# Experts' second products channel-major with the bias in the eviction, and a tail that multiplies by gates spread over the partitions

## What is computed

```python
t = _to_tokens(x)                       # (16, 1024, 128)
t = t + _L0_ffn_ref(_ln_t(t), ...)
...
h = (x_flat @ W_gat).reshape(M, HEADS, NUM_EXPERTS)
...                                     # softmax over each token's edges, sum of the sources' rows
scores = _layernorm(agg, ln_gamma, ln_beta).reshape(M, HEADS, NUM_EXPERTS).mean(1)
topk_s, topk_i = jax.lax.top_k(scores, TOP_K)      # 2 of 4
w = jax.nn.softmax(topk_s, axis=-1)
for ei in range(NUM_EXPERTS):
    g = jnp.where(topk_i == ei, w, 0.0).sum(-1)
    hh = jax.nn.gelu(x @ W1[ei] + b1[ei], approximate=False)
    out = out + g[..., None] * (hh @ W2[ei] + b2[ei])
```

## Time and profile before

| | us |
|---|---|
| timed runs, median of 3 | 4056.19 (4053.61 to 4056.93) |
| profiled execution, first to last instruction | 4750.1 |
| block 1, in the profiled execution | 0 to 2370 |
| block 2, the experts' part and the last rounds | 2370 to 4593 |
| block 3, the gates | 4593 to 4642 |
| block 3, the tail | 4642 to 4750 |

### The profile page before, as it was taken

How to read it: one execution, slowest core, us unless ns; L and a number is a source line. 1 busy time by engine, 2 the same in 40 slices (tenths; PEclk the granted TensorE clock), 3 DMA queues, 4 the chain that set the end, 5 groups by cost and what they waited for, 6 DMA issues and landing times. The chain is left out here.

```text
span 4750.1 us, 30403 instructions
## 1 busy us (share of the span) xinstructions
PE 2949.0 (62%) x8964; PEld 1485.1 (31%) x8964; DVE 3244.3 (68%) x5382; ACT 1526.0 (32%) x2234; POOL 1184.2 (25%) x1252
## 2 busy tenths in 40 slices
PE   6987889999989998866603444334433443345207
PEld 3433333444434443334401222222222222122107
DVE  7899688888887988776445555555544555557587
ACT  2331254444544544455301222212211112112107
POOL 0000000000000000111175445444445555554400
PEclk9989989999999999977756666666566666667559
DMA  4113224544545463856511111111101111011127
GB/s 168 62 58 122 79 72 128 176 147 143 183 123 183 157 209 125 267 185 214 143 17 23 31 31 31 31 31 31 31 22 31 25 31 32 23 14 13 32 109 275
DMA packets 336048, 452.11 MB, mean 95 GB/s; under 512 B 80429, under 2 KB 251832, under 8 KB 326922
## 3 DMA queue, kind: packets, MB, share of 16 engines
q1 hardware_dynamic: 289722, 390.77, 25.2%
q0 software_dynamic: 46160, 59.39, 5.5%
HBM read 340.18 MB, written 109.85 MB: 95 GB/s over the span
## 5 line engine op out<-in xcount | busy, mean ns | idle before, releaser
L1554 POOL DMA_INDIRECT got<-scratch_tab,src_at x1120 | 1065.1, 951 | 341.3 <-issue 341.3
L1508 PE MATMUL hid_ps<-tokens,w 128*128 128x512 f32 x512 | 336.6, 793 | 1068.5 <-ACT hid L1832 580.1
L699 PE MATMUL in_ps<-tokens,w_in 128*128 128x512 f32 x2048 | 939.8, 611 | 24.5 <-ACT zst L906 19.8
L699 PEld LDWEIGHTS in_ps<-tokens,w_in 128*128 128x128 f32 x2048 | 394.8, 197 | 507.6 <-issue 507.6
L1508 PEld LDWEIGHTS hid_ps<-tokens,w 128*128 128x128 f32 x512 | 114.2, 247 | 1192.8 <-ACT hid L1832 604.7
L716 PE MATMUL out_ps<-w_out,act 128*128 128x512 f32 x1024 | 475.7, 608 | 3.9 <-DMA w_out<-in_m_WoutT 3.9
L626 POOL MEMSET tokens<- 1x128 int32 x1 | 0.2, 195 | 1905.6 <-DVE tokens L1098 1905.6
L1097 DVE TENSOR_TENSOR tokens<-tokens 128x1024 f32<-128x1024 f32 x380 | 465.2, 1224 | 11.2 <-ACT tokens L864 10.2
L1524 PE MATMUL y_ps<-w,hid 128*128 128x128 f32 x2048 | 331.0, 314 | 225.5 <-issue 222.0
L1098 DVE TENSOR_TENSOR tokens<-tokens 128x1024 f32<-128x1024 f32 x380 | 464.9, 1224 | 0.0
L1824 ACT ACTIVATE ys<-y_ps 128x512 f32<-128x512 f32 x128 | 76.5, 597 | 1156.5 <-remote 819.5
(11 more groups left out here) (325 smaller groups left out, 4291.7 us busy)
## 6 DMA issues: line engine op xcount, KB each, us to landing
w_out<-in_m_WoutT SPq DMA_DIRECT2D x256, 512.0 KB, 4.5
w_in<-in_m_WinT SPq DMA_DIRECT2D x128, 512.0 KB, 3.9
scratch_y<-ys SPq DMA_DIRECT2D x25, 1024.0 KB
got<-scratch_tab,src_at POOLq DMA_INDIRECT x1120
tokens<-scratch_xt SPq DMA_DIRECT2D x8, 2048.0 KB, 10.0
scratch_sz<-zst SPq DMA_DIRECT2D x64, 256.0 KB, 4.6
gz<-scratch_sz SPq DMA_DIRECT2D x64, 256.0 KB, 4.7
ys<-scratch_y SPq DMA_DIRECT2D x9, 1024.0 KB, 11.6
```

What stands on the lines that cost most here:

```text
L699: last = t_.matmul(in_ps[:, z, :], w_in[:, n % WIN, k, :], xT[:, s % 2, k, :], start=(k == 0), stop=(k == KC - 1))
L1508: last = t.matmul(hid_ps[:, f], w1[:, e, f * P:(f + 1) * P], tokens[:, g * QW:(g + 1) * QW], start=True, stop=True)
L1554: g.indirect_dma_start(got[:, y, t, :], None, tab_d[:, :], bass.IndirectOffsetOnAxis(ap=src_at[:, y, t:t + 1], axis=0))\
```

## The change

In block 2 the second product is turned round. `w2` becomes the stationary operand and the 512 tokens of `hid` the moving one: two matmuls of 512 columns per unit, with channels on the partitions. The bias matmul goes, and `b2`, now one number to a partition, is added by ScalarE's eviction. Nothing else in block 2 changes.

In block 3 the experts' outputs are channel-major already, and the gates must be the same on all partitions and different along the tokens. VectorE splits `by_expert` into three bf16 parts that add up to it (`parts`), SP moves them in twelve DMAs of 32 partitions, so that the gates of 32 chunks lie on 96 partitions (`by_chunk`), and TensorE makes them into `g_ps` per chunk: one bf16 matmul whose stationary operand is a column of `pick`, repeated 128 times, which picks one chunk's three parts, adds them and writes the result to all partitions. VectorE multiplies a whole quarter of four experts in place by `g_ps` (one operation of 128x2048), GpSimd adds the halves in place (experts 0, 1 to 2, 3: 128x1024), VectorE adds the two quarters left into `ost`, then `x2g`. ScalarE has no part in the tail any more. `g_ps` has two places, so TensorE runs two quarters ahead, and VectorE's multiplication too.

```diff
@@ block 2
-            b2 = sb("b2", [1, EXP, P], F32, st)
+            b2 = sb("b2", [P, EXP], F32, st)
...
-                sp.dma_start(b2[:], a["b2"].rearrange("(o e) d -> o e d", o=1)).then_inc(s_mw, 16)
+                with nc.allow_non_contiguous_dma(reason="small parameters, one to a partition"):
+                    sp.dma_start(b2[:], a["b2"].rearrange("e d -> d e")).then_inc(s_mw, 16)
...
-                    t.matmul(y_ps[:, n % 2], ident[0:1, 0:1].to_broadcast([1, P]),
-                             b2[:, e, :].unsqueeze(1).to_broadcast([1, QW // P, P]), start=True, stop=False)
                     t.wait_ge(s_gelu, n + 1)
-                    for c in range(QW // P):
-                        for f in range(FH):
-                            last = t.matmul(y_ps[:, n % 2, c * P:(c + 1) * P], hid[:, n % 2, f, c * P:(c + 1) * P],
-                                            w2[:, e, f, :], start=False,
-                                            stop=(c == QW // P - 1 and f == FH - 1))
+                    for f in range(FH):
+                        last = t.matmul(y_ps[:, n % 2], w2[:, e, f, :], hid[:, n % 2, f], start=f == 0,
+                                        stop=f == FH - 1)
...
-                        s.activation(ys[:, g % SLOTS, e], y_ps[:, n % 2], ACT.Copy).then_inc(s_yc, 1)
+                        s.activation(ys[:, g % SLOTS, e], y_ps[:, n % 2], ACT.Identity,
+                                     bias=b2[:, e:e + 1]).then_inc(s_yc, 1)
@@ block 3, SyncE
-                            sp.wait_ge(s_mix, CH * (q - R + 1))
+                            sp.wait_ge(s_read, q - R + 1)
...
+                sp.wait_ge(s_part, 1)
+                for k in range(P // GROUP):
+                    for x in range(3):
+                        sp.dma_start(by_chunk[x * GROUP:(x + 1) * GROUP, k], parts[k * GROUP:(k + 1) * GROUP, x])\
+                            .then_inc(s_chunk, 16)
@@ block 3, TensorE
...
+                t.wait_ge(s_chunk, 16 * 3 * (P // GROUP))
                 for q in range(NQ_ALL):
                     if q >= 2:
-                        t.wait_ge(s_fin, q - 1)
...
+                        t.wait_ge(s_scaled, q - 1)
                     for c in range(CH):
...
+                        k, i = divmod(CH * order[q] + c, GROUP)
+                        last = t.matmul(g_ps[:, q % 2, c, :], pick[:, i:i + 1].to_broadcast([3 * GROUP, P]),
+                                        by_chunk[:, k, :], start=True, stop=True)
+                    last.then_inc(s_g, 1)
@@ block 3, GpSimd (new)
+                for q in range(NQ_ALL):
+                    y = rings[q % R].rearrange("p (x n) -> p x n", x=2)
+                    g.wait_ge(s_scaled, q + 1)
+                    g.tensor_tensor(y[:, 0], y[:, 0], y[:, 1], ALU.add).then_inc(s_halved, 1)
@@ block 3, VectorE, after the gates
...
+                ck(v.tensor_copy(parts[:, 0], gate))
+                ck(v.tensor_tensor(rest, gate, parts[:, 0], ALU.subtract))
+                ck(v.tensor_copy(parts[:, 1], rest))
+                v.tensor_tensor(parts[:, 2], rest, parts[:, 1], ALU.subtract).then_inc(s_part, 1)
+
+                def scaled(q):
                     if q < NQ_ALL:
...
+                        y = rings[q % R].rearrange("p (e c n) -> p c e n", e=EXP, n=P)
+                        on_chip(v, q)
+                        v.wait_ge(s_g, q + 1)
+                        v.tensor_tensor(y, y, g_ps[:, q % 2].rearrange("p c (e n) -> p c e n", n=P),
+                                        ALU.mult).then_inc(s_scaled, 1)
+
+                scaled(0)
+                scaled(1)
+                for q in range(NQ_ALL):
+                    y = rings[q % R].rearrange("p (e n) -> p e n", e=EXP)
+                    v.wait_ge(s_halved, q + 1)
+                    if q >= 4:
+                        v.wait_ge(s_out[q % 4], 16 * (q // 4))
+                    v.tensor_tensor(ost[:, q % 4, :], y[:, 0], y[:, 1], ALU.add).then_inc(s_read, 1)
+                    scaled(q + 2)
+                    v.wait_ge(s_read, q + 1)
+                    v.wait_ge(s_xg[q % RES], 16 * (q // RES + 1))
+                    v.tensor_tensor(ost[:, q % 4, :], ost[:, q % 4, :], x2g[:, q % RES, :], ALU.add).then_inc(s_fin, 1)
```

More of the change, by code:

```diff
@@ L137 @@
 CH = QW // P
+GROUP = 32
 def image_end(n):
@@ L1924, in program @@
             wide = [P, BINS, H16]
+            agg_n = agg_f.rearrange("p n x -> p (n x)")
+            parts = agg_n[:, 0:3 * QW // 2].bitcast(BF16).rearrange("p (x n) -> p x n", x=3)
+            by_chunk = agg_n[0:3 * GROUP, 3 * QW // 2:7 * QW // 2].bitcast(BF16).rearrange("p (k n) -> p k n", n=QW)
+            rest = e_score[:].rearrange("p n e -> p (n e)")
             found_f = found.rearrange("p n x -> p (n x)")
@@ L1993, in _ @@
                 s.activation(e_score[:], e_score[:], ACT.Exp).then_inc(s_na, 1)
-                s.wait_ge(s_gt, 1)
-                s.activation(g_tok[:], g_ps[:], ACT.Copy).then_inc(s_gt, 1)
-                s.wait_ge(s_gt, 2)
-                for q in range(NQ_ALL):
-                    y = rings[q % R].rearrange("p (e n) -> p e n", e=EXP)
-                    if q >= SLOTS:
-                        s.wait_ge(s_ring[q % R], 16 * (q // R + (1 if q % R >= SLOTS else 0)))
-                    for c in range(CH):
-                        n = CH * q + c
-                        j = CH * order[q] + c
-                        if n >= 8:
-                            s.wait_ge(s_mix, n - 7)
-                        s.activation(first2[:, n % 8], y[:, 0, c * P:(c + 1) * P], ACT.Copy, scale=g_tok[:, 0, j:j + 1])\
-                            .then_inc(s_first2, 1)
-                        s.activation(third[:, n % 8], y[:, 2, c * P:(c + 1) * P], ACT.Copy, scale=g_tok[:, 2, j:j + 1])\
-                            .then_inc(s_da, 1)
             @block.vector
@@ L2023, in _ @@
                     v.memset(rank[:, :, i:i + 1], float(EXP - 1 - i))
+                for x in range(3):
+                    at = slice(x * GROUP, (x + 1) * GROUP)
+                    ck(v.tensor_copy(pick[at, :], ident[at, at]))
                 v.wait_ge(s_nw, 48)
@@ L2070, in _ @@
                 ck(v.reciprocal(vec[1][:], vec[0][:]))
-                v.tensor_tensor(by_expert[:].rearrange("p e n -> p n e"), gates[:], spread(vec[1][:], EXP),
-                                ALU.mult).then_inc(s_nv, 1)
-                v.wait_ge(s_gt, 2)
-                def fourths(q):
-                    if q < NQ_ALL:
-                        y = rings[q % R].rearrange("p (e c d) -> p e c d", e=EXP, d=P)
-                        if q >= SLOTS:
-                            v.wait_ge(s_ring[q % R], 16 * (q // R + (1 if q % R >= SLOTS else 0)))
-                        if q >= 2:
-                            v.wait_ge(s_mix, CH * (q - 1))
-                        j = CH * order[q]
-                        v.tensor_tensor(fourth[:, q % 2].rearrange("p (c d) -> p c d", d=P), y[:, 3],
-                                        g_tok[:, 3, j:j + CH].unsqueeze(2).to_broadcast([P, CH, P]),
-                                        ALU.mult).then_inc(s_four, 1)
@@ new lines, in _ @@
+                ck(v.tensor_tensor(by_expert[:].rearrange("p e n -> p n e"), gates[:], spread(vec[1][:], EXP), ALU.mult))
+                gate = by_expert[:].rearrange("p e n -> p (e n)")
+                ck(v.tensor_copy(parts[:, 0], gate))
[3 more added lines that the diff above has]
+                def scaled(q):
+                    if q < NQ_ALL:
+                        y = rings[q % R].rearrange("p (e c n) -> p c e n", e=EXP, n=P)
[3 more added lines that the diff above has]
+                                        ALU.mult).then_inc(s_scaled, 1)
```

57 lines of the change are left out of this document (13 added, 44 removed).

## The result

The changed kernel takes **4138.57 us** (median; 4135.04 to 4142.39), the kernel before on the same chip 4054.9 (4051.0 to 4056.93). The ratio is 1.0209, 95% interval 1.0196 to 1.0222: 83.7 us slower. The forecast was 91 us slower, 4147 with a range of 4080 to 4165.

What follows compares the result with a forecast made beforehand. Timed loop turns were taken as bound by GpSimd's gathers (82.6 us), so the experts gain 0. A tail start 10 us later and a pace of 5.85 us a quarter add 91 to 4056: 4147 us, range 4080 to 4165.

Steps and rivals of the forecast that it cites:

- 664 of 694 us: Loop and last rounds: gather-bound timed turns of 82.6 us would explain 664 of the 694 us between profiled span and median.
- The experts' part: Loop: 166 us less TensorE work hides under the gathers, and at most 10 us more ScalarE eviction is hidden: 0.
- Rival (b): Loop: experts partly hold timed turns, so the change gains there; 4021 us if a turn were 90; chance 0.10.
- The start: Tail: splitting gates, twelve DMAs and landing put the first multiplication 10 us after the present first product.
- S(0): Tail: S is VectorE's multiplication by the gates; S(0), the first quarter's, was forecast at 4654 us.
- Rival (c): Start of tail: the twelve small DMAs come late once, 10 us on top, 4157 us; chance 0.68 shared with the forecast.
- The pace: Tail: VectorE waiting for GpSimd's addition makes a quarter take 5.85 us, against 2.68 before.
- P: Tail: GpSimd's addition of 128x1024 halves, forecast at 2.35 us a quarter and to go first.
- F: Tail: VectorE's sum with x2g, 0.69 us alone, forecast to wait for GpSimd's addition and last near 3.0.
- A: Tail: VectorE's sum of two halves, 128x512, forecast at 0.69 us, queued behind the sum with x2g.
- the earlier trace: First part: VectorE's addition began 0.23 us before GpSimd's of 2.35, yet lasted 3.14 instead of 0.685.
- Rival (a): Tail: VectorE passes GpSimd twice in a row; pace 3.45, or 3.96 in 17 refilled quarters; +30, 4086 us; chance 0.18.

Runs made afterwards that it cites:

- the kernel before once more: The kernel before, unchanged, profiled a second time: 4050.2 us (one run).
- P after F(q-2): Changed kernel, but GpSimd's addition of halves also waits for VectorE's sum with x2g of two quarters earlier: 4074.9 us, ratio 1.0067.
- P after A: Changed kernel, but GpSimd's addition of halves also waits for VectorE's sum of two halves of the quarter before: 4085.1 us, ratio 1.0070.

## Why the prediction was right, and where it wasn't

**The loop.** The conclusion from 664 of 694 us was right: timed turns are bound by the gathers (82.3 us after, 82.05 in the kernel before once more, 82.6 forecast), and the slow issue belonged to one execution. The experts' part was costed at 0 and measured 1.0002. Each part of the cover was there too: the eviction with a bias takes 0.69 instead of 0.60 and is hidden. Rival (b), that the experts hold a timed turn, is excluded from both sides: 191 us less work for TensorE (166 in the prediction) and 171 us more of it change nothing that can be told from noise. That the profiled turn would shrink "towards 100" was too careful: the slow issue simply didn't come again, and the profiled span of after is the timed one.

**The start.** Forecast 12.1 us from the gates to S(0), measured 13.2. The split took 2.4 instead of 2.8. The twelve issues took 7.55 where I chose 4.6: I had the row for it, 0.6 an issue, and discounted it for the smaller transfers, but these small ones cost 0.63 each. The landing took 1.9 instead of 3.24, 1.3 of it behind the last issue. That the errors nearly cancel is luck. Rival (c) didn't come.

**The pace.** This is the step that was wrong, in its detail and not in its kind. I let P win before F, with F stretched to 3.0 and A free; 5.85 us a quarter. In the trace F passes with 0.68, P waits for it, and A is stretched to 2.83; 5.55. From the quarter shown: S to F 2.19, F 0.68, from F's end to P's 2.20, A's end 0.55 behind that, less 0.08 of overlap with the next S, 5.54. A's own turn of 0.61 behind a stretched F fell away, and F's own turn ahead of P, 0.60, came in its place, which is level. The 0.31 less are the release of 0.10, which now passes beside F, 0.15 of P, which has 2.20 left when F's record ends and not 2.35, and 0.05 in the rest. Either order makes one addition of VectorE wait for a whole P, so the total is near the forecast whichever goes first, and says nothing for the order that I chose. 29 quarters of 0.30 are 9 us under the forecast, and the start is 1 over it: 91 - 9 + 1 = 83.

The Trainium skill, SBUF — State Buffer, section "SBUF: two separate sides", has it that whichever of the two starts first gets the pair for the whole instruction. The prediction set that against the earlier trace rows and chose the row. The trace sides with the page: F, which began 0.16 us first, passes, and the pace of 5.54 is nearer to its 5.75. The row wasn't wrong, it was a case of another kind: behind a DMA issue of GpSimd, where the same meeting gives 5.97. On the one row that spoke against the rule I hadn't asked what GpSimd did just before.

**Rival (a)** had its mechanism wrong for this kernel: VectorE doesn't get past twice, for P's record stands from 0.44 us before A's. Its price was near: where A is let through, as with P after F(q-2), the ratio is 1.0067, 27 us over the kernel before, where the rival said 30. Part of that is luck. It took 3.96 us for each of the 17 refilled quarters, and they ran at 3.40 but for one: 9.5 us less. Against these stand some 8 us that the rival didn't have: 1.1 more ahead of S(0), a first A and a last F that meet P (2.82 and 2.71), and the one quarter of 5.84.

What gives the time back in these kernels is the meeting alone. The sum of what both engines have to do in a quarter didn't change between the change (5.55), P after A (3.65) and P after F (3.40).

## What to carry to other kernels

Before giving GpSimd an elementwise operation to relieve VectorE, write down which VectorE operations with two SBUF inputs will be due while it runs. In these kernels each such meeting of two float32 operations costs the later one the rest of the other, so the help should fall beside an operation that reads PSUM, and one wait can put it there. Ask of any work that an edit removes who waits for it in the timed runs; where a profiled span is far above them, profile the same kernel again before reading a turn from it. And where two rows disagree about an order, look at what each engine did just before, not only at the two that meet.

## What the runs showed of the hardware that was not expected

- A GpSimd DMA issue of 0.54 us under way when VectorE's two-input operation begins lets GpSimd's next addition go first, even 0.33 us after VectorE (A 3.24 us, ratio 1.0246). A fill of 0.52 us in the same place doesn't (A 0.68, ratio 1.0057).
- An operation that waits for the port shows it in a longer record, not as idle time: 2.72 for GpSimd's 2.35, 2.83 for VectorE's 0.68. VectorE's ends 0.55 after GpSimd's, so most of its own 0.68 is done only then. A share of busy time doesn't tell such waiting from work.
- A VectorE multiplication of 128x2048 with one input in PSUM and GpSimd's addition of 128x1024 run side by side at 2.27 and 2.36 us; with GpSimd idle the multiplication takes 2.28, and the addition took 2.35 in the earlier trace rows.
- One execution of 4750 us of a program that otherwise takes 4050, by slow issue on TensorE and ScalarE; it came once, and its cause stays open.
- A DMA from SBUF to SBUF of 32 rows of 1 KB costs SyncE 0.63 us to issue (7.55 for twelve), no less than a load of x2g of 256 KB (0.60).
